# Round of a graph-attention and expert kernel: pool norm on ScalarE, route statistics a round ahead, VectorE's order changed

## What is computed

```python
x = x + _L0_gnn_ref(_layernorm(x), adj, W, a)   # attention over neighbours, then elu
x = x + _L0_ffn_ref(_layernorm(x), ...)         # 6 experts of 3 layers, the 2 best of each node
x = x + _L1_gnn_ref(_layernorm(x), adj, W, a)   # attention again
x = x + _L1_ffn_ref(_layernorm(x), ...)         # 8 experts, chosen for a graph from the mean of its nodes
```

## Time and profile before

| | |
|---|---|
| time, median of 3 runs (range) | 721.52 us (720.93 to 721.79) |
| the profiled execution | 721.59 us, of which the span 719.8 us |
| TensorE matmul busy | 593.0 us (82%) |
| VectorE busy | 455.4 us (63%) |
| ScalarE busy | 393.0 us (55%) |
| GpSimd busy | 290.4 us (40%) |
| mean granted TensorE clock | 0.948 of full speed |
| rounds 2 to 13 | from 116.6 to 467.2 us of the span |
| last phase | from about 554 us |

### The profile page before, as it was taken

How to read it: one execution, slowest core, us unless ns; L and a number is a source line. 1 busy time by engine, 2 the same in 40 slices (tenths; PEclk the granted TensorE clock), 3 DMA queues, 4 the chain that set the end, 5 groups by cost and what they waited for, 6 DMA issues and landing times. The chain is left out here.

```text
span 719.8 us, 15213 instructions
## 1 busy us (share of the span) xinstructions
PE 593.0 (82%) x3969; PEld 481.7 (67%) x4001; DVE 455.4 (63%) x1632; ACT 393.0 (55%) x914; POOL 290.4 (40%) x507
## 2 busy tenths in 40 slices
PE   3468899889898898988989889788522999999993
PEld 2345577667676676767667667566411999999993
DVE  3365668887887877878778787674423144444445
ACT  1234566666665666656666666655421466566552
POOL 4312214553444534535355354343421044444444
PEclk9999999999999999999999999999955899999998
DMA  7404304224042140440412402202001644444422
GB/s 164 111 0 134 112 23 132 67 68 133 3 131 87 45 132 10 122 123 9 132 38 94 132 0 89 87 3 91 0 0 40 185 130 141 142 129 144 144 60 58
DMA packets 74597, 61.98 MB, mean 86 GB/s; under 512 B 7772, under 2 KB 62268, under 8 KB 74562
## 3 DMA queue, kind: packets, MB, share of 16 engines
q1 hardware_dynamic: 61344, 56.14, 26.0%
q10 hardware_dynamic: 13218, 5.42, 2.9%
HBM read 57.13 MB, written 4.41 MB: 85 GB/s over the span
## 5 line engine op out<-in xcount | busy, mean ns | idle before, releaser
L1324 PE MATMUL bank<-w,h2w 128*128 128x128 f32 x768 | 105.4, 281 | 26.1 <-DVE h2w L1008 26.1
L1324 PEld LDWEIGHTS bank<-w,h2w 128*128 128x128 f32 x768 | 96.0, 194 | 31.9 <-DVE h2w L1008 29.8
L798 ACT ACTIVATE h<-bank,b 128x512 f32<-128x512 f32 x96 | 66.0, 688 | 92.7 <-PE bank L1311 92.7
L1311 PE MATMUL bank<-h,w 128*128 128x512 f32 x192 | 104.9, 630 | 1.0 <-ACT h L803 1.0
L803 ACT ACTIVATE h<-bank,b 128x512 f32<-128x512 f32 x96 | 65.7, 684 | 29.3 <-PE bank L1305 28.8
L1008 DVE TENSOR_TENSOR h2w<-h,wide_w 128x512 f32<-128x512 f32 x96 | 70.7, 736 | 16.8 <-ACT h L798 16.8
L1303 PE MATMUL bank<-xnTh,w1h 128*128 128x512 f32 x96 | 69.4, 723 | 0.0
L347 POOL TENSOR_TENSOR x<-x,at_prT 128x512 f32 (+1 forms) x16 | 23.7, 1481 | 80.3 <-DVE at_prT L328 80.3
L101 POOL TENSOR_TENSOR at_var_eps<-at_mean_var,eps 128x4 f32<-128x4 f32 x32 | 13.2, 412 | 102.9 <-DVE at_mean_var L94 102.9
L335 POOL TENSOR_TENSOR at_src<-at_wh,zero 128x8 bf16<-128x8 f32 x32 | 9.8, 306 | 84.0 <-DVE at_wh L303 84.0
L251 PEld LDWEIGHTS wide<-at_wh,at_prT 128*128 128x128 f32 x256 | 33.6, 204 | 13.7 <-ACT at_prT L287 5.2
(11 more groups left out here) (234 smaller groups left out, 1511.5 us busy)
## 6 DMA issues: line engine op xcount, KB each, us to landing
wide_w<-w_scratch SPq DMA_DIRECT2D x96, 256.0 KB, 4.5
mask<-in_L_ffn_W SPq DMA_DIRECT2D x128, 128.0 KB, 2.1
x<-in_x SPq DMA_DIRECT2D x16, 256.0 KB, 6.0
xin<-in_x SPq DMA_DIRECT2D x16, 256.0 KB, 6.1
adj_in<-in_adj SPq DMA_DIRECT2D x16, 256.0 KB, 6.3
out<-at_pr ACTq DMA_DIRECT2D x8, 256.0 KB, 2.7
out<-at_prT ACTq DMA_DIRECT2D x8, 256.0 KB, 2.7
W<-in_L_ffn_W SPq DMA_DIRECT2D x2, 512.0 KB
```

The source lines that it names most:

```text
L798: a.activation(h2[:, e % 2, :], b_h2[:, :], ACT.Relu, bias=b2[:, e:e + 1]).then_inc(h2_ready, 1)
L1311: pe.matmul(b_h2[:, :], w2[:, e, :], h1[:, e % 2, :], start=True, stop=True).then_inc(l2_done, 1)
L1324: last = pe.matmul(b_out[:, s], h2w[:, e % 2, s], w3[:, e, :], start=False, stop=(e == E0 - 1), skip_group_check=True)
```

## The change

- `norm_apply_pool` is gone. ScalarE applies the pool norm instead, with `norm_apply_act` (L116, four activations of 128x128), placed after `attn_act_rows` of attn1 and before relu2(4). The second attention's and other norms stay where they were.
- The route statistics of group i+2 (not i+1) are measured at the end of round i, between max of attn1 and `route_weights`. They wait for the residual of attn0 of the same round. The matching `norm_root` is now the last of GpSimd's round. `norm_apply` for r_xn moves to second place of VectorE's round.
- On VectorE weigh(1), weigh(2), weigh(4) and elu of attn0 move up, max of attn1 moves down, behind elu of attn0 and weigh(4); the pool statistics keep their place between mask and `route_first`, with weigh(2) now ahead of wh of attn1 and the mask.
- On ScalarE pe0 moves ahead of relu2(3), and the elu passes of attn0 ahead of relu1(5).
- TensorE's and SyncE's lists are as before.

```diff
--- before.py
+++ after.py
@@ -129,17 +129,6 @@
         last = v.tensor_scalar(dst(t), src(t), st["mv"][:, t, 0:1], st["rstd"][:, t:t + 1],
                                ALU.subtract, ALU.mult)
     last.then_inc(st["xn_ready"], 1)
-
-
-def norm_apply_pool(st, p, dst, src, const_ready, g):
-
-    settle(p, const_ready)
-    p.wait_ge(st["rstd_ready"], g + 1)
-    p.tensor_tensor(tiles(dst), tiles(src), per_tile(st["rstd"][:, :]), ALU.mult).then_inc(st["scaled"], 1)
-    settle(p, const_ready)
-    p.wait_ge(st["scaled"], g + 1)
-    p.wait_ge(st["shift_step"], 2 * g + 2)
-    p.tensor_tensor(tiles(dst), tiles(dst), per_tile(st["shift"][:, :]), ALU.add).then_inc(st["xn_ready"], 1)
 
 
 def attn_stage(nc, name, bank, parts):
@@ -710,8 +699,6 @@
             def body(i, i0):
                 if live("attn0", i0):
                     attn_pool_split(at0, p, zero, i + 2)
-                if live("route", i0):
-                    norm_root(rn, p, eps, minus_half, i + 1, rn["xn_ready"])
                 if live("attn1", i0):
                     norm_root(at1["norm"], p, eps, minus_half, i - 1, at1["wh_ready"])
                 if live("attn1", i0, -1) and not last(i0):
@@ -725,15 +712,12 @@
                     p.tensor_copy(rstd3[:, bass.ds(g * GG, GG)], pn["rstd"][:, :])
                     p.wait_ge(pn["shift_step"], 2 * g + 2)
                     p.tensor_copy(shift3[:, bass.ds(g * GG, GG)], pn["shift"][:, :])
-                    if last(i0):
-                        return
-                    settle(p, const_ready)
-                    need(p, p_xnT_done, g)
-                    norm_apply_pool(pn, p, p_xn[:, :], x[:, cols(g)], const_ready, g)
                 if live("norm0", i0):
                     norm_root(at0["norm"], p, eps, minus_half, i + 3, at0["wh_ready"])
                 if live("attn0", i0):
                     attn_pool_residual(at0, p, x, x[:, cols(i + 2)], const_ready, i + 2)
+                if live("route", i0, 1):
+                    norm_root(rn, p, eps, minus_half, i + 2, rn["xn_ready"])
                 if i0 == -LEAD["attn0"]:
                     later_constants()
 
@@ -861,28 +845,32 @@
                 if attn0:
                     attn_act_exp(at0, a, i + 2)
 
+                if route:
+                    a.wait_ge(route_step, ROUTE * (i + 1) + 2)
+                    a.activation(pe0[:, :, :], lgd[:, :, :], ACT.Exp).then_inc(pe0_ready, 1)
                 if run:
                     relu2(n + 3, 3)
                 if attn0:
                     attn_act_prT(at0, a, i + 2)
                 if run:
                     relu1(n + 4, 4)
-                if route:
-                    a.wait_ge(route_step, ROUTE * (i + 1) + 2)
-                    a.activation(pe0[:, :, :], lgd[:, :, :], ACT.Exp).then_inc(pe0_ready, 1)
                 if attn1:
                     attn_act_rows(at1, a, i - 1)
+                if pool and not last(i0):
+                    need(a, p_xnT_done, i - 2)
+                    norm_apply_act(pn, a, buf_tile(p_xn), x_tile(i - 2), i - 2)
 
                 if run:
                     relu2(n + 4, 4)
+                if attn0:
+                    attn_act_elu(at0, a, i + 2)
+                if run:
                     relu1(n + 5, 5)
                 if attn1:
                     attn_act_z(at1, a, i - 1)
                 if route:
                     a.wait_ge(route_step, ROUTE * (i + 1) + 7)
                     a.activation(pq[:, :, :], pd[:, :, :], ACT.Exp).then_inc(pq_ready, 1)
-                if attn0:
-                    attn_act_elu(at0, a, i + 2)
                 if pool:
                     pooled(i - 2)
 
@@ -1106,14 +1094,12 @@
                 if attn0:
                     attn_dve_wh(at0, v, i + 2)
                 if route:
-                    measure(rn, i + 1, at0["x_ready"], i + 2)
+                    need(v, r_xnT_done, i + 1)
+                    norm_apply(rn, v, buf_tile(r_xn), x_tile(i + 1), i + 1)
+                if live("route", i0, -1):
+                    weight_low(i)
                 if live("attn1", i0, -1):
                     attn_dve_y(at1, v, i - 2)
-                if live("route", i0, -1):
-                    weight_low(i)
-                if route:
-                    need(v, r_xnT_done, i + 1)
-                    norm_apply(rn, v, buf_tile(r_xn), x_tile(i + 1), i + 1)
                 if live("experts", i0, -1):
                     v.wait_ge(l3_done, i * E0)
                     need(v, at1["x_ready"], i - 2)
@@ -1121,7 +1107,6 @@
                         .then_inc(x_experts_ready, 1)
                 if attn1:
                     measure(at1["norm"], i - 1, x_experts_ready, i, lambda t: xe[:, (i0 + 1) % 2, t * P:(t + 1) * P])
-
                 if run:
                     weigh(n, i, 0)
                 if route:
@@ -1130,6 +1115,9 @@
                     v.wait_ge(xnTh_ready, g + 1)
                     v.tensor_tensor(xnTl[:, par, :], b_misc[:, :], xnTh[:, par, :].bitcast(F32),
                                     ALU.subtract).then_inc(xnTl_ready, 1)
+
+                if run:
+                    weigh(n + 1, i, 1)
                 if live("attn1", i0, -1):
                     attn_dve_elu(at1, v, i - 2)
                     if last(i0):
@@ -1138,18 +1126,15 @@
                             .then_inc(at1["x_ready"], 1)
                 if attn0:
                     attn_dve_max(at0, v, i + 2)
-
-                if run:
-                    weigh(n + 1, i, 1)
                 if live("norm0", i0):
                     measure(at0["norm"], i + 3, x_loaded, 16 * (i + 3) + 16)
+                if run:
+                    weigh(n + 2, i, 2)
                 if attn1:
                     attn_dve_wh(at1, v, i - 1)
                 if live("norm0", i0):
                     make_mask(i + 3, (i0 + 1) % 2)
 
-                if run:
-                    weigh(n + 2, i, 2)
                 if pool:
                     measure(pn, i - 2, at1["x_ready"], i - 1)
                     if last(i0):
@@ -1167,15 +1152,16 @@
                     attn_dve_y(at0, v, i + 2)
                 if run:
                     weigh(n + 3, i, 3)
+                if attn0:
+                    attn_dve_elu(at0, v, i + 2)
+                if run:
+                    weigh(n + 4, i, 4)
                 if attn1:
                     attn_dve_max(at1, v, i - 1)
+                if live("route", i0, 1):
+                    measure(rn, i + 2, at0["x_ready"], i + 3)
                 if route:
                     route_weights(i + 1)
-                if attn0:
-                    attn_dve_elu(at0, v, i + 2)
-                if run:
-                    weigh(n + 4, i, 4)
-                if route:
                     weight_rows(i + 1)
                 if run:
                     weigh(n + 5, i, 5)
```

More of the change, by code:

```diff
@@ L1169, in body @@
                     weigh(n + 3, i, 3)
-                if attn1:
-                    attn_dve_max(at1, v, i - 1)
-                if route:
-                    route_weights(i + 1)
                 if attn0:
@@ L1177, in body @@
                     weigh(n + 4, i, 4)
+                if attn1:
+                    attn_dve_max(at1, v, i - 1)
+                if live("route", i0, 1):
+                    measure(rn, i + 2, at0["x_ready"], i + 3)
                 if route:
+                    route_weights(i + 1)
                     weight_rows(i + 1)
```

## The result

| | before | after |
|---|---|---|
| time, median (range), 4 runs each | 721.22 us (720.25 to 721.79) | 765.9 us (764.48 to 766.69) |
| span of the profiled execution | 719.8 us | 762.7 us |
| TensorE matmul busy | 593.0 us | 607.0 us |
| GpSimd busy | 290.4 us | 253.4 us |
| mean granted clock | 0.948 | 0.921 |

The changed kernel is slower: 1.0619 times the time before, with a 95% interval of 1.0598 to 1.064. The forecast was 750 us with a range of 733 to 762. So the direction is right, the size is 16 us short, and the time lies above the stated range.

A forecast was written before the change was run, and what follows sets the result against it. TensorE bounds the kernel, waiting for h2w, r_xn and wgt. Steady rounds +23.4, start +7.8, end -2.5 make +28.7 on the 719.8 us span; with 1.8 outside it, 750.3, forecast 750 us (733 to 762).

The forecast's parts named there:

- Part 1: Pool norm to ScalarE: removes two GpSimd passes of 1.04 us and 1.7 us on VectorE; four activations cost nothing.
- The 1.97 us before layer 3: TensorE's wait for h2w before layer 3 of expert 3, 1.97 us in the traced round, forecast to go.
- The start: Rounds -2 to 1: later wgt and a split pushed back, less r_xn waits; +7.8 us in sum.
- The new wait: TensorE at the weights transpose (L1330, L1316 after) waits 3.5 us for wgt, behind VectorE's longer queue; start at 283.7.
- the port: GpSimd's residual among VectorE's two-input passes (elu, weigh(4), max1): 0.8 us taken; round grows by 1.3, ends 0.55 and 1.7.
- The lower end of +0.55: Growth of a full-clock round, 28.7 to 29.3 us, from the wgt wait with no port cost.
- the clock: A fall expected after the longer wait in each of 12 rounds, 1.2 us each: +7.8 us, bounds 3 and 12.6.
- the end: Round 14 saves 1.7 us, drain saves 1.2 in round 16 and loses 0.4 in round 15: -2.5 us.
- the sum for the steady rounds: Twelve rounds together: 12 x 1.3 for the longer round plus 7.8 for the clock, +23.4 us.
- Rival (d): Upper ends together: port 1.7 and clock 1.6 a round, start +10; +41 us, 763 us, chance 0.10.
- part 2: Route statistics a round ahead: r_xn follows wh, the 0.79 us wait before L1338 goes; layer 2(1) gains 0.61.
- rival (b): Faster: wgt in time at L1330, rounds of 25.9 us at full clock, 686 us; chance of any gain 0.07.

The follow-up runs named there:

- the kernel with the filled wait: Changed kernel plus 16 more matmuls of 128x512 on TensorE ahead of L1316 in rounds 0 to 14, result unaffected: 742.5 us, ratio 1.0287.
- first part alone: Kernel before with only the pool norm moved to ScalarE, behind the rows of attention 1, every order kept: 701.33 us, ratio 0.9723.

## Why the prediction was right in direction and short in size

**Step by step, what held.** Part 1 frees prob and over: 0.18 and 0.31 us. The 1.97 us before layer 3 are gone. The wait for r_xn is gone, and layer 2(1) then waits for h1 (0.26 us at 319.22). The four activations cost nothing on the way to elu: they end just as relu2(4) starts, 1.96 us behind the aggregate (300.28 less 298.32), as before the change:

```profile
298.60 1.65 ACT L120 ACTIVATE p_xn<-x,pool_shift,pool_rstd 128x128 f32 x4
300.28 0.69 ACT L782 ACTIVATE h<-bank,b 128x512 f32<-128x512 f32 x1
```

The start was +7.8 as forecast, with L1316 of round -1 at 58.73 ("near 58"), but that it fits to the digit is partly luck: the forecast was 5.7 + 1.2 + 0.9 for rounds -1, 0 and 1, and it came as 6.3 + 0.3 + 1.2.

**The new wait.** The chain was right in each link but one. From the aggregate of attention 0 to max1's first pass I had 5.07 us (275.00 to 280.07); it is 5.07 (298.32 to 303.39). From the statistics to L1316 I had 1.06 for 282.64 to 283.7, and 1.25 for the statistics, in all 2.3; it is 2.30 (305.78 to 308.08). Between them, max1's two passes, I had 1.32 us and it is 2.39.

**First term that was mis-sized: the port.** I took 0.8 us, the middle between "max1 gets in first" and "the residual gets in first". The trace shows the second: GpSimd's residual starts at 303.12, while weigh(4) holds VectorE until 303.48. Then, as I read it, the residual gets its turn, and max1, issued at 303.39, ends only at 305.14, 0.55 us behind the residual's end at 304.59. It takes 1.06 us too long, and so it does in all 13 rounds in which the two meet. This was the upper end, which the prediction gave to the rule of the Trainium skill (page "SBUF — State Buffer", section "Who interferes with whom") that the order of issue decides. By that rule, the trace agrees: 303.12 is before 303.39, and 1.75 us stands against 0.69. There was a reason in the rows to take this end: the two-input passes stood close behind each other, with 0.60 us from start to start, and the residual's request fell 0.25 us after the end of elu, inside weigh(4); max1 could only ask later. With it and two smaller things (0.12 us more from L1316 to layer 2(0) in the kernel with the filled wait, 4.54 against 4.42; some 0.1 not placed) a round without a fall is 30.51 us rather than 30.0. That is +1.8 a round, where I had +1.3: 6 us over 12 rounds, of which the port itself (1.06 in place of 0.8) makes about 3. The lower end of +0.55 was too low in any case: it charges nothing for the port, though the cheaper of the prediction's own two cases cost 0.5.

**Second term that was mis-sized: the clock.** I took 1.2 us for a fall, and 12 falls. The mechanism and the count were right, not the price. My price came from the kernel before, whose six falls are all of 3.4 us, like this one:

```profile
310.15:313.56 3.41, 3.41 (x16) 3.02 (x15) 2.98 (x10) 1.50 (x10) 0.94 (x1) 0.50 0.00 0
```

In the kernel after, a fall of 6.8 us and one of 3.4 us take turns from the wait of round 3 on, as the windows above show for one of each, and so do the rounds behind them: 32.75 us (308.08 to 340.83), then 31.93 (340.83 to 372.76). Against the 30.51 us of a round at full clock the long fall costs 2.2 us and the short one 1.4; before, a fall cost 1.1. In the mean it is 1.7, and the term is 12 x 1.7 - 6 x 1.1 = +13.8, where I had +7.8 with an upper bound of 12.6. That a longer wait could lengthen the fall, and not only make it more frequent, was missing in the bounds. The five long falls began 0.8 to 1.7 us before the end of the wait, and six of the seven short ones at its end or up to 0.5 us behind it; the seventh began 0.7 us before. Why the two lengths alternate stays open.

**Third: the end.** I had -1.7 for round 14; it is +0.3 (26.46 us against 26.20). Two things were left out. The wait of 5.1 us at the end of round 13 brings a fall of the clock for round 14 too (0.50 from 501.52 to 504.93 above). And L1316 still waits there, since max1 stands ahead of `route_weights` in that round as well:

```profile
528.55 0.31 PE L1316 MATMUL wide<-ident,wgt 128*88 128x128 f32 x1 [1.84 <-DVE wgt L1053]
```

The drain gave 1.1 us where I had 0.8. Together the end is -0.8 in place of -2.5.

The three terms add up: 6 + 6 + 1.7 = 13.7 of the 14.2 us that the span is longer than forecast (42.9 against 28.7). So the step that failed is the sum for the steady rounds, with its two terms: the round without a fall, 12 x 1.3, which came as 12 x 1.8, with the stall at the port as its largest error, and the clock, +7.8, which came as +13.8. Two of the prediction's own signs show it: it wanted rounds of 29.8 to 31.7 us and a wait of 3.5 to 4.6, and they are 32.2 and 4.66. Behind it is one habit: where two ends were known, I took the middle, twice. For the port the rows gave a reason to take the upper end. For the clock the prediction said itself that 1.7 us of work are lost and that all behind is on the chain, and still took 1.2. Rival (d), "upper ends together, 763 us, chance 0.10", is in the main what happened: the round without a fall 1.8, clock 1.7, start 7.8. A last 1.4 us of the 15.9 are the median of the runs above the profiled one.

**What the prediction didn't see** is how much the two parts were worth by themselves. It said that part 1 takes away 1.97 us and part 2 0.61, and its rival (b) worked out 686 us for the case that wgt comes in time. The kernel of both parts in the old order takes 690, and with `route_weights` put early 671.

## What to carry to other kernels

When instructions are moved ahead on an in-order engine, ask for each one that they pass who waits for it: here `route_weights`, 1 us of work that TensorE needs next, was passed by nearly 5 us of work and a wait of 1.25 us, none of it needed as soon, and with it a gain of 32 us became a loss of 45. Put the short chain that the busiest engine waits for first, and work for the next round (statistics a round ahead) last. Where a bound depends on which of two engines gets a port first, read from the rows which one asks first, instead of taking the middle.

## What the runs showed of the hardware

- In all 13 rounds of the kernel after in which they meet, a GpSimd pass that starts while VectorE runs a two-input pass (303.12, with VectorE busy to 303.48) gets its turn before VectorE's next such pass (issued at 303.39), though VectorE's passes follow each other without a gap. In the profile the blocked one is not shown as idle but as long: 1.75 us in place of 0.69 (1.76 in the kernel with `route_weights` early). With the GpSimd pass gone it is 0.68 on average.
- A fall of the clock has no fixed price, and a wait of one length does not settle whether it comes. With a wait of 1.97 us in most rounds (1.4 at the least) it came in six of twelve rounds, lasted 3.4 us and cost 1.1. With a wait of 3.43 us (3.9 in round 1) it came in ten of twelve. With a wait of 4.66 us (5.1 in round 1) it came in all twelve, lasted 6.8 or 3.4 us and cost 2.2 or 1.4. With no wait above 0.88 us in the steady rounds (first part alone, where 0.80 to 0.88 are the wait for r_xn) or 0.95 us (filled wait) the clock stayed at 1.00 through all of them.
- 16 matmuls that do nothing for the result, in 3.98 us of the wait, kept the clock at 1.00 and won 23.4 us.
